# Three waits of TensorE for VectorE, in front of FFN pieces, are left out of the written-out node blocks

## The reference

```
xn = layernorm(x); xp = xn @ W                       # 12500 x 256, 4 heads of 64
alpha = leaky_relu(a_src[src] + a_dst[dst])          # per edge and head
ex = exp(alpha - max of the target)
out = segment_sum(xp[src] * ex, dst) / segment_sum(ex, dst) + bias
x = x + elu(out)
z = layernorm(x)
weights = z @ wr + br                                # one number per node
h = gelu(z @ w1 + b1)                                # 256 -> 1024
y = h @ w2 + b2                                      # 1024 -> 256
x = x + z + y * weights     # the y term only for the nodes of the top half by weight
```

## Time and profile before

| | us |
|---|---|
| median of 3 runs | 2186.64 (2186.37 to 2191.46) |
| profiled execution | 2193.97 |
| its span | 2192.2 |
| TensorE busy in the span | 1883.2 (86%) |
| VectorE busy | 1533.1 (70%) |
| ScalarE busy | 1154.9 (53%) |
| GpSimd busy | 1525.6 (70%) |
| mean granted TensorE clock | 0.931 of full |

### The profile page before, as it was taken

How to read it: one execution, slowest core, us unless ns; L and a number is a source line. 1 busy time by engine, 2 the same in 40 slices (tenths; PEclk the granted TensorE clock), 3 DMA queues, 4 the chain that set the end, 5 groups by cost and what they waited for, 6 DMA issues and landing times.

```text
span 2192.2 us, 29093 instructions
## 1 busy us (share of the span) xinstructions
PE 1883.2 (86%) x9507; PEld 1547.8 (71%) x9508; DVE 1533.1 (70%) x3416; ACT 1154.9 (53%) x1672; POOL 1525.6 (70%) x1626
## 2 busy tenths in 40 slices
PE   8945888898899889888888888889889889888887
PEld 6734777777677777777777776767677777777775
DVE  5556776677677667767767777777667667777776
ACT  4543555555555555555555555555555555555533
POOL 2367777777777777777777777777777777777710
PEclk9977999999999999999999999999999999999988
DMA  8854455455455555554555555455545545555457
GB/s 281 296 167 136 134 145 146 133 146 146 136 142 146 146 137 142 146 141 133 146 146 137 142 146 146 138 140 147 146 132 145 146 135 142 144 147 138 135 226 284
DMA packets 157136, 340.11 MB, mean 155 GB/s; under 512 B 46645, under 2 KB 73937, under 8 KB 155698
## 3 DMA queue, kind: packets, MB, share of 16 engines
q0 software_dynamic: 75088, 208.19, 35.0%
q1 hardware_dynamic: 74706, 116.59, 16.7%
q10 hardware_dynamic: 7184, 13.41, 1.6%
HBM read 299.38 MB, written 38.68 MB: 154 GB/s over the span
## 4 chain that ended last, share of the span: by engine, by line
POOL 49%; issue 22%; PE 12%; DMA 11%; ACT 3%; DVE 1%; POOLq 1%; DVEq 0%; SPq 0%; ACTq 0%
POOL rows L710 49%; DMA rows<-node_rows,ends 10%; PE ag_ps L972 4%; ACT rows L854 3%; PE ag_ps L1097 2%; PE y_ps L1080 2%; PE h_ps L1061 2%; POOLq L410 1%; PE ag_ps L1168 1%; PE ag_ps L1169 0%; DVE rows L1443 0%; DMA steps_of_rows<-in_L_gnn_att_dst 0%; DMA selfr<-in_dst,edge_block 0%; PE xl_ps L1001 0%; PE tr_ps L1001 0%
## 5 line engine op out<-in xcount | busy, mean ns | idle before, releaser
L710 POOL DMA_INDIRECT rows<-node_rows,ends x1563 | 1484.1, 950 | 493.2 <-issue 449.9
L1097 PE MATMUL ag_ps<-rows,oh 128*128 128x260 f32 x3518 | 835.4, 398 | 26.1 <-DVE rows L1443 25.6
L1097 PEld LDWEIGHTS ag_ps<-rows,oh 128*128 128x128 f32 x3518 | 690.3, 200 | 172.6 <-DVE rows L1443 51.8
L1061 PE MATMUL h_ps<-xnT,w1s 128*128 128x256 f32 x1568 | 457.1, 443 | 215.9 <-DVE zz L1424 201.1
L1443 DVE TENSOR_TENSOR rows<-rows,xl_ps 128x512 f32<-128x512 f32 (+3 forms) x392 | 503.1, 1346 | 47.2 <-ACT rows L874 47.2
L1061 PEld LDWEIGHTS h_ps<-xnT,w1s 128*128 128x128 f32 x1568 | 327.7, 217 | 291.6 <-DVE zz L1424 209.8
L1080 PE MATMUL y_ps<-w2s,hT 128*128 128x256 f32 x1568 | 368.8, 384 | 11.5 <-DVE oh L1405 7.6
L1080 PEld LDWEIGHTS y_ps<-w2s,hT 128*128 128x128 f32 x1568 | 296.2, 191 | 71.6 <-DVE oh L1405 25.9
L1424 DVE TENSOR_TENSOR zz<-rows,edge_dm 128x72 f32<-128x72 f32 x98 | 22.8, 233 | 447.8 <-DMA rows<-node_rows,ends 432.7
L854 ACT COPY rows<-rows 128x780 f32<-128x780 f32 x97 | 81.6, 842 | 403.5 <-DMA rows<-node_rows,ends 403.5
L1405 DVE TENSOR_TENSOR oh<-xl_ps,dloc 128x2304 f32<-128x2304 f32 x98 | 249.0, 2541 | 0.0
(11 more groups left out here) (245 smaller groups left out, 1528.9 us busy)
## 6 DMA issues: line engine op xcount, KB each, us to landing
spare<-dst SPq DMA_DIRECT2D x97, 288.0 KB, 4.7
rows<-node_rows,ends POOLq DMA_INDIRECT x1563, 2.9
selfr<-node_rows SPq DMA_DIRECT2D x98, 130.0 KB, 3.0
base<-in_x SPq DMA_DIRECT2D x14, 896.0 KB, 7.0
base<-in_x SPq DMA_DIRECT2D x49, 256.0 KB, 3.3
ffn_rows<-yb ACTq DMA_DIRECT2D x48, 256.0 KB, 4.8
node_rows<-base SPq DMA_DIRECT2D x13, 910.0 KB, 5.5
base<-in_x_turned SPq DMA_DIRECT2D x14, 384.0 KB, 7.5
```

The costliest lines, as they stand in the source:

```text
L710: pool.indirect_dma_start(out=rows[:, b, t, :], out_offset=None, in_=table, in_offset=bass.IndirectOffsetOnAxis(ap=ends[:, b, t, 0:1], axi ...
L1061: last = nc.tensor.matmul(h_ps[:, m * PAIR:(m + 1) * PAIR], w1s[:, c, n * P:(n + 1) * P], xnT[:, c, :], start=(c == 0), stop=(c == DC - 1))
L1097: product = nc.tensor.matmul(ag_ps[b][:, 0:ROW], oh[:, b, t, :], rows[:, b, t, :], start=(t == 0), stop=False)
```

## The change

In the tensor engine's window body three conditional waits go. No instruction is added, removed or put elsewhere on any engine.

```diff
                 if known(w, 4) and not (isinstance(w, int) and w == NW - 1):
-                    if isinstance(w, int):
-                        pe.wait_ge(zs_ok, w + 1)
                     hidden(w - 4, b, i - 2, (1,))
...
                 if known(w, 4):
                     ffn_out(w - 4, b, i - 2, (0,))
-                    if isinstance(w, int) and w + 1 < NW:
-                        pe.wait_ge(oh_ok, w + 2)
                     ffn_out(w - 4, b, i - 2, (1,))
                 if known(w, 3) and not (isinstance(w, int) and w == NW - 2):
-                    if isinstance(w, int) and w + 2 < NW:
-                        pe.wait_ge(dm_ok, w + 2)
                     hidden(w - 3, 1 - b, i - 2 + b, (0,))
```

## The result

| | before | changed |
|---|---|---|
| median of 20 runs each | 2185.54 us (2179.35 to 2191.46) | 2189.13 us (2184.59 to 2195.81) |
| span of the profiled execution | 2192.2 | 2187.6 |
| its mean granted clock | 0.931 | 0.921 |
| TensorE busy in it | 1883.2 | 1871.6 |

The ratio is 1.0016 (95% interval 1.0009 to 1.0024): slower, by 3.6 us, where 13 were forecast. The spans of the single profiled executions stand the other way round by 4.6 us, so what one of them totals cannot carry a difference of this size; what they show is where idle time stands.

What follows compares the result with a forecast made beforehand. GpSimd's gathers were taken as the bound, 20.0 us per window. 28 long clock drops at 0.85 us minus 6.9 of stalls gave +17, at 0.58 +9; +13 was taken: 2186.64 + 13 = 2200 us, range 2186 to 2214.

Steps and rivals of the forecast that it cites:

- The bound: GpSimd's gathers set the loop's pace: 1.25 us each, mostly 16 per window, 20.0 us; other engines have slack.
- Where the idle goes: TensorE's waits move into one 3.66 us idle before the sum, which then waits for the first weighed piece.
- a window on time: Window like that with `zz` at 1000.68: 2.37 us TensorE idle before the next `zz`, forecast to become 3.66 us.
- What the idle does to the clock: TensorE's clock falls after long idles: 28 long and 27 short drops forecast over 93 windows.
- the forecast's own classes of idle: TensorE idles: under 1.3 us, 0 of 12 dropped; 1.7 to 2.9, 35 of 56; 3.3 and more, 13 of 13.
- The cost of a drop on TensorE: Time lost between held piece and output piece: 2.65 us for a long clock drop, 1.5 for a short one.
- The slack of GpSimd: Output piece done at `zz` + 14.7, its waiting gather at `zz` + 16.55: 1.87 us, so only short drops fit.
- the price of a drop: GpSimd's stall at the output piece's hold: 0.85 us per long drop; today's stalls put at 0.58 us each.
- The sum: 28 long drops' cost minus today's 6.9 us of stalls: +17 or +9, taken as +13 us, giving 2200 us.
- No change: Rival: GpSimd's pace hides all clock drops, as a short one fits its slack; 2187 us, chance 0.23.
- Faster: Rival: the held piece runs earlier at full clock, so GpSimd's 6.9 us of stalls go; 2179 us, chance 0.07.
- third rival: Much slower: every window on time drops long, every second window, and short drops hurt 15-gather windows; 2220 us, chance 0.12.

Runs made afterwards that it cites:

- e7: Changed kernel; GpSimd waits for the sum of two windows ago instead of the FFN output piece, and holds for the sum's thirds come later: 2185.95 us, ratio 0.9989.
- e8: Kernel before; GpSimd waits for the sum of two windows ago instead of the output piece, with later holds for the sum's thirds: 2185.23 us, ratio 0.9993.
- e5: Changed kernel with GpSimd waiting for the FFN output piece one gather sooner: 2211.75 us, ratio 1.0108 to the kernel before.
- e6: Kernel before with GpSimd waiting for the FFN output piece one gather sooner: 2198.76 us, ratio 1.0044.
- freed kernels: The two kernels of e7 and e8, the changed one and the one before, with GpSimd's holds loosened: ratios 0.9989 and 0.9993.
- e11: e7 plus 26 extra matmuls per window, results unused, in TensorE's idle in front of the sum: ratio 0.9987 to the kernel before.
- e4: Changed kernel plus 26 extra matmuls per window, results unused, in TensorE's idle in front of the sum: ratio 0.9998 to the kernel before.
- e2: Kernel before with only the `oh_ok` wait left out: ratio 0.9993.

## Why the prediction was right in kind and wrong in size

- **The bound.** Right: GpSimd's gathers set the pace, 1.25 us each. e7 and e8 differ by 0.02 of clock, and not in time that can be told.
- **Where the idle goes.** Right: 3.66 us reckoned for a window on time, 3.69 read; what TensorE waits for next is the first weighed piece, as forecast.
- **What the idle does to the clock.** Right as a rate. By the forecast's own classes of idle the changed kernel has no drop behind the 13 under 1.3 us; 29 short ones behind the 39 between 1.7 and 2.9; 9 short and 19 long ones behind the 28 of 3.3 us and more. 19 of 28 is the forecast's 9 of 13. The count was too high, 28 long drops against 19: the middle class of idles, where windows mostly stand behind a short drop, led to another short drop in 29 of 39 cases and not in 32 of 56, so more windows stayed in it and fewer came back on time.
- **The cost of a drop on TensorE.** Right: 2.65 forecast, 2.7 read; for a short one 1.5 forecast, 1.6 read (sums of 9.84 us).
- **The slack of GpSimd, and with it the price of a drop.** This is the step that failed. "The gather that waits for it stands at 1017.23, `zz` + 16.55" gave 1.87 us, and from it 0.85 us for each long drop. That gather does stand there, but the window gathered in front of it has 15 gathers and not 16. I took it for one of 16 because the `zz` steps were 20.2 us apart, and those were 15 gathers and a last transfer that came late. The chain of waits of the kernel before has both, the last transfer of the window with `zz` 1000.68 and of the one with 1020.89; they start 18.74 us apart, 15 times 1.25:

```profile
997.24 2.72 DMA rows<-node_rows,ends
```

```profile
1015.98 4.19 DMA rows<-node_rows,ends
```

  With 16 gathers the held one comes 1.25 us later, 17.7 us after `zz` (652.92 - 635.18). The slack is 17.7 - 14.7, some 3.1 us before rounding, and 2.8 after the step from product to gather: a drop of 2.7 us fits. With 15 gathers it is 1.6 us and does not. Those are 14 windows of 92, so the price came to 7.7 / 19 = 0.41 us per long drop and not 0.85. That price also left out the holds for the sum, which take 4.5 of the 7.7 us, in the same windows. e5 and e6 come near to the forecast's premise: with the hold one gather sooner the slack is about 1.8 us in the usual window (and less than 1 in those of 15), and the two kernels stand 13.0 us apart by the medians, 14 by the ratios, with some 5 us of uncertainty; that this is so close to the forecast's +13 is in part luck.
- **The sum.** Both of its factors were too large, the price the more: 28 x 0.41 - 6.9 is +4.6 us, 19 x 0.85 - 6.9 is +9.2. With both as measured it is 7.7 - 6.9 = +0.8, which is what the two traces show; the medians say 3.6. The freed kernels say where that is: freeing brings the changed kernel from 1.0016 to 0.9989, 5.9 us, and the one before from 1 to 0.9993, 1.5 us. The difference is 4.4 us, with over 3 us of uncertainty; it agrees with a price of 3.6 us that lies wholly in GpSimd's holds, and does not prove that nothing else has a part. The 6.9 us of stalls in the trace of the kernel before are more than the 1.5 us that freeing gave back (2.3 by the medians), so that execution probably stalled more than most, and they should not have stood in the sum as what every execution pays.
- **The rivals.** "No change" argued with the right mechanism (a short drop fits, and windows with more gathers have more slack; it gave the added slack to those with 17, where those with 16 have it already), and the time falls in its 2183 to 2192: 0.16% is under the 0.3% that I had said could be told from no change, though 20 runs do tell it. "Faster" fell: the held piece does run at full clock now, and stalls are still there, since the sum itself is slow (1.43 - 0.30 = 1.13 us at 824.44). The rule of the Trainium skill (TensorE: Matmul & The Clock Gate, section "Why this matters for your kernels"), which the forecast tied to its third rival and which warns of gaps over about 3 us, is not borne out by this trace if it is read as leaving shorter ones free: 29 of 39 idles of 1.7 to 2.9 us were followed by a drop.

## What to carry to other kernels

An engine that runs ahead behind a hold is safe by a slack, and the slack is a distribution, not a number: before it goes into a sum, read the held instruction in several periods and count what is in each, since two deviations can hide one another in the spacing. Merging TensorE's idle into one piece lowered its clock, and that had a price only through who waits for TensorE: here from nothing to 24 us at the same mean clock of 0.922, by where GpSimd's holds stood. The cheap repair was at the hold (wait for what is really needed, the sum and not the output piece), not at the clock.

## What the runs showed of the hardware that was not expected

Work without a purpose in TensorE's idle (26 bf16 matmuls of 248 columns per window) raised the mean granted clock from 0.921 to 0.977 and cost nothing that can be measured (e11 against e7). And the gather itself is not the same length in each execution. The costliest group of the profile for the changed kernel and for e4:

```profile
L710 POOL DMA_INDIRECT rows<-node_rows,ends x1563 | 1481.8, 948 | 494.7 <-issue 449.4
```

```profile
L710 POOL DMA_INDIRECT rows<-node_rows,ends x1563 | 1488.4, 952 | 488.6 <-issue 454.7
```

6.6 us of busy time more for the same 1563 gathers; e2 has 1487.4 too, with no fill, and e11 with fill 1483.0, so it is not the matmuls. It goes into the time: from first to last gather e4 takes 1964.0 us and e11 1957.9, and 5.4 of these 6.1 us are the gathers' busy time. It is as large as the effects looked for here, so a single execution cannot carry them. What makes a gather longer in one execution than in another is open.
